# Gate and up projections of a feed-forward layer by Strassen's product of 2 x 2 blocks

## The reference

```python
x = x + LN(attn(LN(x)))          # attn mixes rows of LN(x) by relu'd scores
x = x + LN(ffn(LN(x)))
# ffn, t tokens (rows), h = 2048, i = 5632:
g = einsum('th,ih->ti', xf, gate_w) * gate_s
u = einsum('th,ih->ti', xf, up_w) * up_s
out = einsum('ti,hi->th', silu(g) * u, down_w) * down_s
```

## Time and profile before

| | |
|---|---|
| time, median of 3 runs (lowest to highest) | 1125.2 us (1125.04 to 1125.5) |
| profiled execution, its own time | 1125.52 us |
| its span on the slowest core, core 6 | 1124.0 us |
| TensorE matmuls busy | 1072.5 us, 95% |
| VectorE busy | 392.8 us, 35% |
| ScalarE busy | 222.4 us, 20% |
| DMA, mean over the span | 90 GB/s |

### The profile page before, as it was taken

How to read it: one execution, slowest core, us unless ns; L and a number is a source line. 1 busy time by engine, 2 the same in 40 slices (tenths; PEclk the granted TensorE clock), 3 DMA queues, 4 the chain that set the end, 5 groups by cost and what they waited for, 6 DMA issues and landing times.

```text
span 1124.0 us, 12647 instructions; the slowest of 8 cores (1121.3 to 1124.0 us)
## 1 busy us (share of the span) xinstructions
PE 1072.5 (95%) x5101; PEld 495.7 (44%) x5204; DVE 392.8 (35%) x507; ACT 222.4 (20%) x305; POOL 52.0 (5%) x98
## 2 busy tenths in 40 slices
PE   3899999999999999999999999999999999999993
...
GB/s 254 78 1 117 171 183 129 76 136 127 42 62 122 47 64 116 57 60 109 67 58 100 75 57 97 73 63 96 67 73 94 59 82 94 49 131 20 1 119 181
DMA packets 18632, 101.33 MB, mean 90 GB/s; under 512 B 2192, under 2 KB 2320, under 8 KB 9744
## 3 DMA queue, kind: packets, MB, share of 16 engines
...
...
## 4 chain that ended last, share of the span: by engine, by line
PE 88%; ACT 4%; DVE 4%; issue 3%; DMA 1%; DVEq 0%; ACTq 0%; SPq 0%
PE ps L696 27%; PE ps L707 27%; PE ps L749 26%; PE ps L430 5%; PE ps L399 2%; DMA xr<-xtop 1%; ACT lc L531 1%; DVE xr L494 1%; ACT pc L321 1%; ACT lc L454 1%; DVE acc L732 0%; PE ps L381 0%; PE ps L349 0%; ACT lnfT L327 0%; PE ps L359 0%
## 5 line engine op out<-in xcount | busy, mean ns | idle before, releaser
L696 PE MATMUL ps<-lnfT,wr 128*128 128x512 bf16 x1378 | 316.2, 379 | 1.6
L707 PE MATMUL ps<-lnfT,wr 128*128 128x512 bf16 x1379 | 316.1, 379 | 1.5
L749 PE MATMUL ps<-dwb,hdn 128*128 128x512 bf16 x1382 | 313.9, 379 | 1.4
L767 DVE TENSOR_TENSOR acc<-acc,ps 128x2048 f32<-128x2048 f32 x70 | 160.2, 2288 | 187.8 <-PE ps L749 187.8
L721 DVE SCALAR_TENSOR_TENSOR hdn<-ps,cpks,sg 128x512 bf16<-128x512 f32 x88 | 66.1, 751 | 426.5 <-PE ps L707 417.9
L701 ACT ACTIVATE sg<-ps,cpks 128x512 bf16<-128x512 f32 x88 | 60.5, 687 | 773.0 <-PE ps L696 773.0
L749 PEld LDWEIGHTS ps<-dwb,hdn 128*128 128x128 bf16 x1408 | 137.8, 98 | 166.1
L707 PEld LDWEIGHTS ps<-lnfT,wr 128*128 128x128 bf16 x1408 | 137.8, 98 | 166.1
L696 PEld LDWEIGHTS ps<-lnfT,wr 128*128 128x128 bf16 x1408 | 137.7, 98 | 165.7
L430 PE MATMUL ps<-att,xT 128*128 128x512 bf16 x498 | 118.4, 379 | 0.9
L430 PEld LDWEIGHTS ps<-att,xT 128*128 128x128 bf16 x512 | 49.5, 98 | 57.8 <-issue 0.8
...
## 6 DMA issues: line engine op xcount, KB each, us to landing
wr<-gu POOLq DMA_DIRECT2D x44, 1024.0 KB, 9.7
dwb<-dw POOLq DMA_DIRECT2D x44, 512.0 KB, 15.6
xr<-x SPq DMA_DIRECT2D x8, 1024.0 KB, 8.6
y<-xr SPq DMA_DIRECT2D x8, 1024.0 KB, 4.9
y<-acc POOLq DMA_DIRECT2D x6, 1024.0 KB, 8.3
x1r<-y SPq DMA_DIRECT2D x2, 1024.0 KB, 6.0
xr<-xtop SPq DMA_DIRECT2D x2, 512.0 KB, 8.4
...
```

What stands on the lines that cost most here:

```text
L696: t = pg.pe(lambda e, ht=ht: e.matmul(ps[:, gb, :], wr[:, s, 0, ht * P:(ht + 1) * P], lnfT[:, h, ht, :], start=(ht == 0), stop=(ht == HT - ...
L707: t = pg.pe(lambda e, ht=ht: e.matmul(ps[:, ub, :], wr[:, s, 1, ht * P:(ht + 1) * P], lnfT[:, h, ht, :], start=(ht == 0), stop=(ht == HT - ...
L749: t = pg.pe(lambda e, gi=gi, li=li, hc=hc: e.matmul(ps[:, banks[hc], :], hdn[:, gi % HS, tt * P:(tt + 1) * P], dwb[:, gi % DS, hc * MQ:(hc ...
L767: acc_t[tt] = pg.dv(lambda e: e.tensor_tensor(dst, dst, src, ALU.add), [t, acc_t[tt]])
```

## The change

For each pair of tiles and for gate or up alone, the product weights (2 tiles x 2 halves of the hidden dimension) by tokens (2 halves of hidden x 2 halves of tokens) is a 2 x 2 product of blocks. It is written in Winograd's form of Strassen's product, with 7 products of 8 matmuls instead of 8:

- Step m = 2 .. 43: even m is the gate of tiles m and m+1, odd m the up of tiles m-1 and m. t_gu is packed by such steps, one load of 1 MB (bf16) each, into slots of seven parts: four loaded (A11, A12, A21, A22), and S1, S2, S4 added by four VectorE sums per step (combos; S3 overwrites A21).
- The tokens live in bop, also seven parts: ltr writes B11, B21, B12, B22, and for token tiles of the second half adds three VectorE sums (T1, T2, T4) each; T3 is one large sum that overwrites B12 once the plain units are done.
- product(m, k) is 8 matmuls into one of four PSUM banks (a ring of 4, 6, 7 and bank 5). ScalarE copies P1, U2 and U3 to tmp in f32; VectorE adds another bank to each copy (joined_up). The results feed Silu (even m) or the gated product into hdn (odd m).
- Tiles 0 and 1 are computed plainly, as 4 units plain(gi, h, n).
- Slots: wr 3 steps instead of 6 tiles, hdn 8 instead of 12, dwb 6 instead of 8, xT 3 instead of 8. The buffer of DMA descriptors is given as 4096 bytes a partition. Down weights of tiles 42 and 43 go to places of their own (dwx0, dwx1), freed by steps 41 and 42.
- In a step stand: product 6, 5, a down, 7, product 1 of the next step, 4, product 2 of the next step, a second down, 3, then the load of step m+3. At the last step of a block the down loads follow it. The downs keep their form: the same matmuls and the same accumulation.

The core of the diff (in the main loop only added and kept lines):

```diff
-WS = 6
-HS = 12
-DS = 8
+WS = 3
+HS = 8
+DS = 6
+NM = IT
+A11, A12, A21, A22, S1, S2, S4 = range(7)
+S3 = A21
+B11, B21, B12, B22, T1, T2, T4 = range(7)
+T3 = B12
+PROD = {1: (A11, B11), 2: (A12, B21), 3: (S4, B22), 4: (A22, T4),
+        5: (S1, T1), 6: (S2, T2), 7: (S3, T3)}
...
-    nc = bass.Bass("TRN2", target_bir_lowering=False)
+    nc = bass.Bass("TRN2", target_bir_lowering=False,
+                   dynamic_dma_scratch_size=4096)
...
-    t_gu = nc.dram_tensor("gu", [IT, P, 2, D], F32, kind="ExternalInput")
+    t_gu = nc.dram_tensor("gu", [NM, P, 4, R], F32, kind="ExternalInput")
...
+    ((bop,), (_, bcb, amixb, gT, Xn, V), (x1r, junk)) = views(
+        57344,
+        [("bop", [P, 7, 8, MQ], BF16)],
+        [("padA", [P, 32768 // 4], F32),
+         ("bcb", [P, 2, 2, J], BF16), ("amixb", [P, 2, J], BF16),
+         ("gT", [P, 2, J], BF16),
+         ("Xn", [P, 2, D], BF16), ("V", [P, 2, D], BF16)],
+        [("x1r", [P, 2, D], F32), ("junk", [P, D], BF16)])
+    ((_, xT, xr), (wr, dwb), (dwx1, _, dsB, dwx0)) = views(
+        67584,
+        [("padB", [P, 22528 // 4], F32), ("xT", [P, 3, NT, P], BF16),
+         ("xr", [P, 4, D], F32)],
+        [("wr", [P, WS, 7, R], BF16), ("dwb", [P, DS, D], BF16)],
+        [("dwx1", [P, D], BF16), ("padC", [P, 24576 // 4], F32),
+         ("dsB", [P, D], F32), ("dwx0", [P, D], BF16)])
...
+        if dt >= 4:
+            for out, in0, in1 in ((T1, B12, B11), (T2, B22, T1), (T4, B21, T2)):
+                bop_t[out] = pg.dv(lambda e, out=out, in0=in0, in1=in1:
+                                   e.tensor_tensor(
+                    bop[:, out, :, o:o + P], bop[:, in0, :, o:o + P],
+                    bop[:, in1, :, o:o + P], ALU.subtract),
+                    [*lnfT_t[0].values(), *lnfT_t[1].values(),
+                     bop_t.get(in1)])
...
+    def load_w(m, after=()):
+        s = m % WS
+        w_ld[m] = pg.dma("gpsimd", f"w{s}", wr[:, s, 0:4, :],
+                         t_gu.ap()[m], after)
+    def dw_at(gi):
+        return {IT - 2: dwx0, IT - 1: dwx1}.get(gi, dwb[:, gi % DS, :])
...
+    def plain(gi, h, n):
+        for m in range(2):
+            bk = (2 * n + m) % 4
+            for ht in range(HT):
+                t = pg.pe(lambda e, bk=bk, m=m, ht=ht: e.matmul(
+                    ps[:, bk, :],
+                    wr[:, m, gi * 2 + ht // 8,
+                       (ht % 8) * P:(ht % 8 + 1) * P],
+                    bop[:, (B11, B21, B12, B22)[2 * h + ht // 8], ht % 8, :],
+                    start=(ht == 0), stop=(ht == HT - 1)),
+                    [w_ld[m], *lnfT_t[h].values(), *tok_bank[bk]]
+                    if ht == 0 else (), sig=(ht == HT - 1))
+            w_free[m] = t
+            if m == 0:
+                c = silu(gi, 2 + n % 2, ps[:, bk, :], [t])
+            else:
+                c = gated(gi, h, 2 + n % 2, ps[:, bk, :], [t])
+            tok_bank[bk] = (c,)
...
+    RING, CB = (4, 6, 7), 5
+    cmb, st, tmp_free, tmp_n = {}, {}, {}, [0]
+    def combos(m):
+        u = wr[:, m % WS, :, :]
+        def one(out, in0, in1, op, *needs):
+            def f():
+                cmb[(m, out)] = pg.dv(lambda e: e.tensor_tensor(
+                    u[:, out, :], u[:, in0, :], u[:, in1, :], op),
+                    [w_ld[m], *(cmb[(m, n)] for n in needs)])
+            return f
+        return [one(S1, A21, A22, ALU.add),
+                one(S2, S1, A11, ALU.subtract, S1),
+                one(S4, A12, S2, ALU.subtract, S2),
+                one(S3, A11, A21, ALU.subtract)]
+    def copied(m, name, bk, t):
+        k = tmp_n[0] % 4
+        tmp_n[0] += 1
+        c = pg.ac(lambda e: e.copy(tmp[:, k, :], ps[:, bk, :]),
+                  [t, *tmp_free[k]])
+        st[(m, name)] = (k, c)
+        tok_bank[bk] = (c,)
+    def joined_up(m, name, bk, t, li, h):
+        k, c = st[(m, name)]
+        a = pg.dv(lambda e: e.tensor_tensor(
+            tmp[:, k, :], tmp[:, k, :], ps[:, bk, :], ALU.add), [t, c])
+        tok_bank[bk] = (a,)
+        tmp_free[k] = (used(m, li, h, tmp[:, k, :], a),)
+    def used(m, li, h, src, after):
+        gi, q = 2 * (m // 2) + li, 2 * li + h
+        if m % 2 == 0:
+            return silu(gi, q, src, [after])
+        return gated(gi, h, q, src, [after])
+    def product(m, k):
+        a_bk = RING[2 * (m - 2) % 3]
+        b_bk = RING[(2 * (m - 2) + 1) % 3]
+        bk = {2: CB, 5: b_bk, 3: b_bk}.get(k, a_bk)
+        ws, bs = PROD[k]
+        need = [w_ld[m], *tok_bank[bk], cmb.get((m, ws)), bop_t.get(bs),
+                *(lnfT_t[bs // 2].values() if bs < T1 and k != 7 else ())]
+        for c in range(8):
+            t = pg.pe(lambda e, c=c: e.matmul(
+                ps[:, bk, :], wr[:, m % WS, ws, c * P:(c + 1) * P],
+                bop[:, bs, c, :], start=(k in (1, 2, 5) and c == 0),
+                stop=(c == 7), skip_group_check=(k not in (1, 2))),
+                need if c == 0 else (), sig=(c == 7))
+        if k == 1:
+            copied(m, "P1", bk, t)
+        elif k == 2:
+            joined_up(m, "P1", bk, t, 0, 0)
+        elif k == 6:
+            copied(m, "U2", bk, t)
+        elif k == 5:
+            st[(m, "P5")] = t
+            tok_bank[bk] = (t,)
+        elif k == 7:
+            copied(m, "U3", bk, t)
+            joined_up(m, "U3", b_bk, st[(m, "P5")], 1, 1)
+        elif k == 4:
+            tok_bank[bk] = (used(m, 1, 0, ps[:, bk, :], t),)
+        else:
+            joined_up(m, "U2", bk, t, 0, 1)
+            w_free[m] = t
...
+    load_w(2, [t0_tok[(7, 3)], spill[4], lnf_done[4]])
+    plain(0, 0, 0)
     norm_a_dv(last)
     norm_a_ac(last)
     x1(last)
     square2(last)
+    plain(1, 0, 1)
     ltr(last - 1)
     norm_b_dv(last)
     norm_b_ac(last)
+    for k in range(4):
+        tmp_free[k] = (ltr_t[6],)
+    product(2, 1)
+    product(2, 2)
+    for gi in range(DS):
+        i = 5 + gi // 2
+        load_dw(gi, [spill[i], lnf_done[i]])
     ltr(last)
+    tmp_free[2] = tmp_free[3] = (ltr_t[7],)
+    plain(0, 1, 2)
+    for f in combos(2):
+        f()
+    plain(1, 1, 3)
+    bop_t[T3] = pg.dv(lambda e: e.tensor_tensor(
+        bop[:, T3, :, :], bop[:, B22, :, :], bop[:, B12, :, :], ALU.subtract),
+        [w_free[1], *lnfT_t[1].values()])
+    load_w(3, [w_free[0]])
+    load_w(4, [w_free[1]])
+    for m in range(2, NM):
+        b = next(k for k in range(NB) if 2 * (m // 2) < BASE[k] + BLKS[k])
+        n = m - BASE[b]
+        cs = combos(m + 1) if m + 1 < NM else [lambda: None] * 4
+        d = b > 0 and n < 4
+        product(m, 6)
+        cs[0]()
+        product(m, 5)
+        cs[1]()
+        if d:
+            down(b - 1, 2 * n)
+        product(m, 7)
+        cs[2]()
+        if m + 1 < NM:
+            product(m + 1, 1)
+            product(m, 4)
+            cs[3]()
+            product(m + 1, 2)
+            if d:
+                down(b - 1, 2 * n + 1)
+            product(m, 3)
+            if m + 3 < NM:
+                load_w(m + 3, [w_free[m]])
+        if d and n == 3:
+            for li in range(BLKS[b - 1]):
+                gi = BASE[b - 1] + li + DS
+                if gi < IT - 2:
+                    load_dw(gi, [hd_last[gi - DS]])
+        if m == NM - 3:
+            load_dw(IT - 2, [w_free[NM - 3]])
+            ds_ld = pg.dma("sync", "dsb", dsB[:, :], t_ds.ap(),
+                           [w_free[NM - 3]])
+        if m == NM - 2:
+            load_dw(IT - 1, [w_free[NM - 2]])
```

More of the change, by code:

```diff
@@ new lines, in build_nc, with silu, gated @@
+    sl_t, hd_t, hd_gi, hd_last = {}, {}, {}, {}
+    sg_free = {q: tuple(pc_free) for q in range(4)}
+    acc_t = {}
+    def silu(gi, q, src, after):
+        sl_t[q] = pg.ac(lambda e: e.activation(
+            sg[:, q, :], src, AF.Silu, scale=cpk[:, C_GS + gi:C_GS + gi + 1]),
+            [*after, *sg_free[q]])
+        return sl_t[q]
+    def gated(gi, h, q, src, after):
+        if gi < HS:
+            free = x1_tok[6 + gi // 4]
+        else:
+            free = hd_last[gi - HS]
+        t = pg.dv(lambda e: e.scalar_tensor_tensor(
+            hdn[:, gi % HS, h * MQ:(h + 1) * MQ], src,
+            cpk[:, C_US + gi:C_US + gi + 1], sg[:, q, :],
+            ALU.mult, ALU.mult), [*after, sl_t[q], free])
+        sg_free[q] = (t,)
+        hd_gi[(gi, h)] = t
+        return t
@@ L734, in acc_part, with down_mm @@
             [part_t[k], acc_t[tt]])
-    def down(b, tt, banks, hc_outer=False, split=False):
-        nb = BLKS[b]
-        order = ([(li, hc) for hc in range(4) for li in range(nb)] if hc_outer
-                 else [(li, hc) for li in range(nb) for hc in range(4)])
+    def down_mm(b, tt, banks, order, sig):
         for k, (li, hc) in enumerate(order):
             gi = BASE[b] + li
-            first, last = k == 0, k == len(order) - 1
-            w = []
-            if first:
-                w = [gu_last[(b, tt // 4)],
-                     *(t for bk in banks for t in tok_bank[bk])]
-            if tt == 0:
-                w.append(dw_ld[gi])
```

(55 more changed lines are left out.)

139 lines of the change are left out of this document (19 added, 120 removed).

## The result

The changed kernel takes 1153.54 us (median of four runs, 1152.16 to 1161.88); the kernel before, run beside it, 1125.35. The ratio is 1.027, with an interval of 1.021 to 1.033: slower. The forecast was 1171 with a range of 1142 to 1194, so direction and mechanism came out, and the price was 17.5 us too high: 46 us of rise forecast, 28 measured. The profiled execution took 1152.16 us.

The account below looks back on a forecast made before the run. TensorE was taken as the bound. Span 1124.0 - 72.5 (matmuls saved) + 12.9 (start) + 85.6 (down waits) + 20 (clock) = 1170.0 us, forecast as 1171, with a range of 1142 to 1194.

Parts of the forecast that it names:

- What goes: Steps 2 to 43: 56 matmuls each instead of 64, 336 fewer in all, 72.5 us off TensorE's path.
- VectorE and ScalarE: Inside steps: VectorE busy 10.5 us and ScalarE 3.4 of 19.0, neither filling up, so TensorE stays the bound.
- The cost of 0: Inside steps: added VectorE and ScalarE work delays TensorE by 0, at most 0.4 us in each of 42 steps.
- rival 3: Longer still: upper-bound loads and clock loss, 1199 us, or VectorE's upper bound with missed covers, 1188; chance 0.10.
- The down wait: First down of blocks 1 to 8: TensorE waits for dwb loads, 10.7 us each, 85.6 us; sign 70 to 102.
- the arrival sum: Down loads behind a gate/up load: 8.9 us landing plus 3.5 per down load; waits below 7 us would break it.
- The clock: After each of eight down waits TensorE restarts at half clock, costing 2.5 us each, 20 us; bounds 0 and 3.3 each.
- rival 2: At the down waits: they come but the clock stays or recovers at once, 1149 us, band 1130 to 1155; chance 0.18.
- The start: Start of the feed-forward part: idle time for lc and tokens, a late load and clock loss, 12.9 us, bounds 7 and 17.
- load 3: Gate/up load for step 3: lands 6.2 us after plain(1,1) ends, wanted at 5.2, so 1.0 us of wait.
- Load 43: Last step's gate/up load, behind load 42 and four down loads: a wait of 0 to 1 us, taken 0.
- Rival 4: From 190 us on the granted clock falls to 13/16 under the sums' non-zero values: 1365 us; chance 0.03.

Follow-up runs that it names:

- Kernel 2: The changed kernel loading only the first six tiles' down weights and using them for all other tiles (output not the reference's): 1067.11 us, ratio 0.948.
- Kernel 8: The changed kernel with first-needed down loads ahead of gate/up, slots freed by their own last reader, plus three of four weight sums per step done twice: 1069.3 us.
- Kernel 3: The changed kernel with 30 extra unused matmuls before tile 2 in the first down of blocks 1 to 8: 1148.58 us, ratio 1.020.

## Why the prediction was right, and where its sizes were off

**What goes: right.** 42 steps of 56 matmuls, 18.99 us a step with two downs, 72.5 us. Kernel 2 confirms the base without waits.

**VectorE and ScalarE: right.** Inside the steps TensorE waits for neither of them; the sum of weights took the 0.69 us that I had chosen between 0.69 and 1.22. VectorE is busy for 10.5 us of a step of 18.99 (391.71 to 410.70 on core 5), as forecast, but by luck: a step has two gated products and not 1.5, which makes the sum 10.9, and neighbouring instructions overlap by some 0.1 us in the trace. Kernel 8 bears out the slack. The cost of 0 holds, and the VectorE half of rival 3 falls.

**The down wait: right in place, count and form, too long by 1.3 to 3.3 us.** There are two waits in each of eight blocks. In all they are 66.9 us on core 5, just under the 70 to 102 that the prediction gave as its sign, and 54 to 55 on the cores that lead their pairs, 6.8 us a block, below the 7 that it said would break the arrival sum. The delay of a block, which also holds the slow four matmuls of tile 2, can be worked out from the trace. Tile 3 is wanted 6.0 - 0.7 = 5.3 us after the gate/up issue, its load is issued 1.06 after that, so the delay is its landing less 4.26. On core 5 the landings were 16.4, 14.9, 13.6, 13.6, 13.3, 12.5, 12.5 and 12.3, and the delays add to 75.0 us, 9.4 a block; on the cores that lead their pairs the landings were mostly 11.7 to 12.3, and the delay 7.4 to 8.0. The step that failed is the arrival sum, with 8.9 + 2 x 3.5 from rows in which the cores load together (the gate/up loads of cores 6 and 7 near 415 us are issued 0.2 us apart). The DMA view of the changed kernel, two loads each (gate/up, then the second down load behind it) of core 5 at 339.2 us, core 5 at 864.4 and core 4 at 851.6:

```profile
wr<-gu POOLq DMA_DIRECT2D x1, 1024.0 KB, 10.1
...
dwb<-dw POOLq DMA_DIRECT2D x1, 512.0 KB, 16.4
...
wr<-gu POOLq DMA_DIRECT2D x1, 1024.0 KB, 8.5
...
dwb<-dw POOLq DMA_DIRECT2D x1, 512.0 KB, 12.5
...
wr<-gu POOLq DMA_DIRECT2D x1, 1024.0 KB, 8.1
...
dwb<-dw POOLq DMA_DIRECT2D x1, 512.0 KB, 12.0
```

One down load behind another takes (12.0 + 1.06 - 8.1) / 2 = 2.5 us when core 4 is 12.8 us ahead of its partner, and (16.4 + 1.06 - 10.1) / 2 = 3.7 when core 5 loads 3.5 us behind core 4. I had 3.5 for all of them. That the partner's loads make the difference is inferred from when loads land and was not tried alone. For it speaks that of cores 0 and 1, 2 and 3, 4 and 5, and 6 and 7 each has one core with early and one with late landings, and that on core 5 gate/up loads land after 8.4 or 8.5 us too once the two are over 12 us apart. The Trainium skill, "HBM Reference", section "Specifications (TRN2)", says that two cores share a domain: a core alone reaches about 425 GB/s, and with both streaming each gets about 358. Reading 1.05 MB in 2.5 us is 420 GB/s and agrees with the first figure; 1.05 MB in 3.7 us is 283, under the second.

**The clock: right that it falls, 20 us was too much.** Of the 87.9 us on core 5, 75.0 are the delays, so 12.9 are left for the clock, 1.6 a block. Kernel 3 gives 1.1 behind the short waits. I took 2.5 from the start of the span, out of a range of 0 to 3.3; there the sixteen matmuls behind the gap took 6.08 us for 3.62. The first block fits that: the four of tile 3 take 1.86 for 1.02 and fifteen behind them 4.91 for 3.40, 2.4 us. In other blocks full clock comes back sooner. The length of the wait alone does not set this: in blocks 3, 4 and 5, with first waits of 7.71, 7.71 and 7.41 us, 1.2, 0.6 and 2.1 us are left for the clock by the same sum. What does is not shown. Core 5, seventh block, from its timeline:

```profile
875.63 1.86 PE L836 MATMUL ps<-dwb,hdn 128*128 128x512 bf16 x4 [7.03 <-DMA dwb<-dw]
878.06 1.87 PE L836 MATMUL ps<-dwb,hdn 128*128 128x512 bf16 x4 [0.57 <-DMA dwb<-dw]
879.73 5.62 PE L798 MATMUL ps<-bop,wr 128*128 128x512 bf16 x24
```

The 24 matmuls of the last row take 0.3 us more than the 5.34 of a warm group, and the four before them 0.8 more than 1.02: 1.1 us. By the time alone rival 2 would have won: 1153.54 lies in its band (1130 to 1155) and 1.5 us below the forecast's own (1155 to 1187). Its mechanism is not what happened: on core 5 the clock fell in every block, and it cost 12.9 us.

**The start: right, and a gain at the end that I had not seen.** The prediction had 7.7 us idle for lc, 3.5 for the tokens, 1.0 for load 3 and 2.5 for the clock. Core 5:

```profile
204.17 3.62 PE L798 MATMUL ps<-bop,wr 128*128 128x512 bf16 x16
208.59 2.29 DVE L570 TENSOR_TENSOR bop<-bop 128x1024 bf16<-128x1024 bf16 x3
213.53 2.10 ACT L545 ACTIVATE lc<-xr,ng,r 128x2048 bf16<-128x2048 f32 x1 [0.36 <-DVE ng L542]
215.77 1.86 PE L555 MATMUL ps<-idms,lc 128*128 128x128 bf16 x16 [7.99 <-ACT lc L545]
220.13 16.32 PE L733 MATMUL ps<-bop,wr 128*128 128x512 bf16 x64 [2.50 <-ACT bop L340]
```

The idle times are 8.0, 2.5 and 1.9, less the 1.8 of before. The 64 matmuls take 2.3 us over the 13.98 of 64 at 2.4 GHz (0.38 + 63 x 0.2158), and the 16 transposes 1.86 for the 1.05 of the earlier trace rows, 0.8 more. That makes 13.7 for the start; another 0.4 came before it (204.17 for 203.76). The span has only 11.0 left because its end is shorter: from the last matmul to the end it is 15.8 us on core 5 where it was 19.4, and all of that lies behind the first of the last six stores, 8.8 us for 12.6. Before and after:

```profile
1111.37 6.14 SPq L76 DMA_DIRECT2D y<-acc  x6
1141.59 6.16 SPq L86 DMA_DIRECT2D y<-acc  x6
```

13.7 + 0.4 - 3.6 = 10.5 of the 11.0. Why the last stores take 8.8 us on this core, and 11.9 on core 0 (from 1128.5 to 1140.4), was not tried. Load 43 and the down of the last blocks brought no wait, as taken.

**Rival 4** is out: with eight cores on these products the clock is 1.00 inside the blocks (the window of 380 to 400 us).

**In figures:** the waits 75.0 for 85.6 and the clock 12.9 for 20 on core 5, the start and all else 11.0 for 12.9: 98.9 for 118.5, and the span 1150.4 for 1170.0. So 10.6 of the 19.6 us are the arrival sum, in which every load was priced by the crowded case, 7.1 are the price of the clock, taken from one restart, and 1.9 the rest.
